# Cross-attention: the reciprocal of the second query tile's sums taken between the next pair's two maxima, not behind them

## The reference, cut to what matters

```python
q = q * scale
sim = jnp.einsum('bhid,bhjd->bhij', q, k)
attn = jax.nn.softmax(sim, axis=-1)
out = jnp.einsum('bhij,bhjd->bhid', attn, v)
out = out.transpose(0, 2, 1, 3).reshape(b, -1, INNER)
out = jnp.einsum('bnf,fd->bnd', out, Wout)
```

## Time and profile before

| what | value |
|---|---|
| median of 3 runs | 651.12 us (650.49 to 651.89) |
| the profiled execution's own time | 651.96 us |
| its span, from the first to the last instruction | 649.9 us |
| TensorE busy | 567.8 us, 87% |
| VectorE busy | 495.3 us, 76% |
| ScalarE busy | 419.7 us, 65% |
| GpSimd busy | 322.9 us, 50% |
| mean granted TensorE clock | 0.95 of full speed |

### The profile page before, as it was taken

One profiled execution on the slowest core, in us unless ns is written; L12 is line 12 of the kernel. 1 busy time (PEld: TensorE's weight loads), 2 busy tenths in 40 slices (PEclk: granted clock), 3 DMA queues, 4 the chain that ended last, 5 costly groups with the idle time before them and its releaser, 6 DMA issues. The chain is left out here.

```text
span 649.9 us, 11036 instructions
## 1 busy us (share of the span) xinstructions
PE 567.8 (87%) x3380; PEld 444.1 (68%) x3380; DVE 495.3 (76%) x1030; ACT 419.7 (65%) x1024; POOL 322.9 (50%) x606
## 2 busy tenths in 40 slices
PE   2959999999999889999987748899986599999996
PEld 1737868777677677787766636665554578888885
DVE  4757877886889587888689625998984479999995
ACT  2538777786767657777667415898883365656653
POOL 1345766785678765787667646466965100000000
PEclk9989999999999899999989865999998599999999
DMA  7020000000100000000000002002220000000001
GB/s 263 2 59 1 2 33 2 1 2 2 32 2 2 2 1 1 1 2 2 2 0 2 2 21 73 1 3 86 85 86 2 0 1 1 1 1 1 2 0 33
DMA packets 14393, 13.14 MB, mean 20 GB/s; under 512 B 2048, under 2 KB 13696, under 8 KB 14336
## 3 DMA queue, kind: packets, MB, share of 16 engines
q1 hardware_dynamic: 14032, 12.41, 6.0%
q10 hardware_dynamic: 304, 0.03, 0.0%
HBM read 11.92 MB, written 0.52 MB: 19 GB/s over the span
## 5 line engine op out<-in xcount | busy, mean ns | idle before, releaser
L1071 POOL TENSOR_SCALAR attn_probs<-attn_probs,rinv 128x512 f32<-128x512 f32 x128 | 87.4, 695 | 29.5 <-DVE rinv L975 29.5
L848 ACT ACTIVATE attn_probs<-bank,bias 128x512 f32<-128x512 f32 x128 | 87.3, 687 | 10.0 <-DVE bias L968 10.0
L984 DVE TENSOR_TENSOR pT_lo<-bank,pT_hi 128x512 fp32r<-128x512 f32 x128 | 87.4, 685 | 7.2 <-ACT pT_hi L864 5.8
L701 PE MATMUL bank<-ident,attn_probs 128*128 128x128 f32 x512 | 77.6, 285 | 12.5 <-POOL attn_probs L1071 11.8
L960 DVE TENSOR_REDUCE neg_max<-bank 128x1 f32<-128x512 f32 x128 | 82.0, 682 | 6.7 <-PE bank L686 6.7
L864 ACT ACTIVATE pT_hi<-bank 128x512 fp32r<-128x512 f32 x128 | 73.3, 594 | 15.3 <-PE bank L701 15.0
L701 PEld LDWEIGHTS bank<-ident,attn_probs 128*128 128x128 f32 x512 | 57.4, 143 | 36.5 <-POOL attn_probs L1071 21.0
L731 PE MATMUL bank<-pT_hi,vals 128*128 128x256 f32 x256 | 67.6, 295 | 2.2 <-DVE pT_lo L984 1.4
L731 PE MATMUL bank<-pT_lo,vals 128*128 128x256 f32 x256 | 65.6, 288 | 0.0
L1885 ACT ACTIVATE act_hi<-act_f 128x512 fp32r<-128x512 f32 x56 | 35.4, 633 | 43.4 <-DVE act_f L1926 43.3
L731 PEld LDWEIGHTS bank<-pT_hi,vals 128*128 128x128 f32 x256 | 49.9, 195 | 4.3 <-issue 1.7
(11 more groups left out here) (311 smaller groups left out, 1614.5 us busy)
## 6 DMA issues: line engine op xcount, KB each, us to landing
ctx_raw<-in_ctx SPq DMA_DIRECT2D x4, 512.0 KB, 4.8
wkv_raw<-in_L_xattn_Wkv SPq DMA_DIRECT2D x2, 1024.0 KB, 10.4
gu_raw<-in_L_ffn_w_gate SPq DMA_DIRECT2D x4, 448.0 KB, 3.6
gu_raw<-in_L_ffn_w_up SPq DMA_DIRECT2D x4, 448.0 KB, 4.4
dn_raw<-in_L_ffn_w_down SPq DMA_DIRECT2D x4, 448.0 KB, 5.4
x<-in_x SPq DMA_DIRECT2D x1, 512.0 KB, 6.8
wq_raw<-in_L_xattn_Wq SPq DMA_DIRECT2D x1, 512.0 KB, 10.3
wout_raw<-in_L_xattn_Wout SPq DMA_DIRECT2D x1, 512.0 KB, 12.1
```

Source lines behind the costliest of these rows:

```text
L701: last = pe.transpose(t_bank[half][:, j * N + t * P:j * N + (t + 1) * P], probs[:, g % 2, i, t, kt * P:(kt + 1) * P], k.ident[:, :])
L848: act.activation(probs[:, g % 2, i, t, :], score_bank(G, i)[:, :], ACT.Exp, bias=bias[:, t, h:h + 1], scale=X_SCALE, accum_out=row_sum[:, ...
L984: dve.tensor_tensor(pT_lo[:, i, 2 * half:2 * half + 2, :], t_bank[half][:, :].rearrange("p (j n) -> p j n", j=2), f(pT_hi[:, i, 2 * half:2 ...
L1071: pool.tensor_scalar(probs[:, g % 2, i, t, :], probs[:, g % 2, i, t, :], rinv[:, t, h:h + 1], 1.0, ALU.mult, ALU.mult).then_inc(p_norm_s, 1)
```

## The change

In VectorE's list the reciprocal of pair `s+1`, tile 1, moves ahead of one instruction: the second maximum of pair `s+2`, tile 0. Nothing else is touched; the instructions, their operands and their semaphores are the same.

```diff
                 probs_tail(s, 1, 0)
                 context_tail(s, 0)
                 maximum(s + 2, 0, 0)
+                inverse_sum(s + 1, 1)
                 maximum(s + 2, 0, 1)
-                inverse_sum(s + 1, 1)
                 shift(s + 2, 0)
                 context_tail(s, 1)
```

## The result

The changed kernel takes 646.67 us (median of 6 runs, 646.28 to 647.35) where the kernel before took 650.7 (median of 6 runs beside it): ratio 0.9938, 95% interval 0.9925 to 0.9951, a gain of 4.0 us. The forecast was 649.0 with a range down to 646.8: the sign was right, the size about half. The profiled execution took 646.28, with a span of 644.2 us (651.96 and 649.9 before).

The account below looks back on a forecast made before the run. TensorE was taken to bound the kernel, full in quiet steps, elsewhere waiting for GpSimd's normalisations. 1.00 + 1.10 + 0 + 0 + 0 = 2.1 us off 651.96 gave 649.9, and 649.0 for the median; range 646.8 to 651.5.

Parts of the forecast that it names:

- The chain at 187 us and its like: Early-sum steps at 187, 243, 329, 356 us: normalisation 0.60 us earlier, 0.35 reaching TensorE (0.30 at 356); 1.00 us together.
- 187 to 207 and 275 to 295: Three steps and their twin: an unstretched shift brings VectorE and the sum 0.33 us forward; about 0.55 us each, 1.10 together.
- 340, 347 and 356 us: 340 and 347 put at 0, between a gain of 0.13 + 0.45 and a loss of 0.2; 356 at 0.30 us.
- the prediction's nine waits, all for a normalisation: TensorE's cross-attention waits for GpSimd's normalisation: ten, 11.8 us in all; the last pair's 2.3 us left out.
- its bound of 0.60 for this step: At 356 us the step could give at most 0.60 us.
- Late sums at 0: In 14 steps GpSimd's sum is 0.3 us or more late; TensorE's backlog covers the late tail: 0, uncovered 9.4 us.
- The port: Moved shift falls among GpSimd's normalisations on the shared port, waits 0.12 us, ends with the first normalisation: 0.
- that rival (the shift behind the second normalisation): Each step's shift waits 0.66 us more: 656.7 us, or 653 if in a third of the steps; chance 0.11.
- The clock: Rival: shorter waits may keep TensorE at 2.4 GHz at 329 and 356 us, 0.83 + 0.43 us more; 647.3; chance 0.11.
- Its outer bound: No step gives more than the wait it has or 0.60 us, together 4.4 us off: 646.8.

Follow-up runs that it names:

- before_again: The kernel before, unaltered, run once more for a second profile: 650.17 us, ratio 0.9999.
- late_sums_only: Kernel before with the reciprocal moved only in the 14 pairs whose GpSimd sum is later than the first maximum: 652.16 us, ratio 1.0026.
- before_look1: The kernel before, unaltered, first of three more executions with a profile: 650.51 us.
- before_look3: The kernel before, unaltered, third of three more executions with a profile: 652.01 us.
- not_last_four: Kernel before with the reciprocal moved in all pairs but 27 to 30: 647.43 us, ratio 0.996.
- fill_all_before: Kernel before, old order, with unread matmuls filling TensorE's waits at pairs 14, 19, 22, 27 and 30: 649.06 us, ratio 0.9977.
- fill_long_waits: Kernel before, old order, with unread matmuls filling TensorE's waits at pairs 19, 27 and 30 alone: 649.3 us, ratio 0.9977.
- fill_waits: Kernel before, old order, with unread matmuls in TensorE's waits at pairs 27 and 30: 647.16 us, ratio 0.995.
- all_but_three: Kernel before with the reciprocal moved everywhere but in pairs 15, 23 and 28: 645.17 us, ratio 0.9921.
- after_look1: The changed kernel, unaltered, one more execution with its profile: 646.99 us.
- fill_all_after: Changed kernel with unread matmuls in what is left of TensorE's waits at pairs 14, 19, 22, 27 and 30: 646.87 us, ratio 0.9943.

## Why the prediction was half right

**The chain at 187 us and its like: right.** The prediction moved the normalisation 0.60 us, let 0.35 of it reach TensorE, and named the tail as the next late thing. Pairs 19 and 27 gave 0.36 to 0.42, and the second group of transposes starts 0.14 us behind the end of the tail, 185.72 to 185.86, as the 0.15 of the earlier trace rows had it.

**187 to 207 and 275 to 295: right in mechanism, a little too high.** The shift of 189.53 is no longer stretched (0.14 us at 188.03). It was not alone: where the prediction has "the others take 0.16", eleven shifts of the second tile took 0.44 to 0.67 us in the kernel before (pairs 5, 13, 15 to 17, 20, 21, 23 to 25, 28), each beside GpSimd's long subtraction, as this one of pair 16:

```profile
199.96 0.67 DVE L968 SCALAR_TENSOR_TENSOR bias<-neg_max,s0n 128x2 f32<-128x2 f32 x1
...
199.87 0.74 POOL L1101 TENSOR_TENSOR o_lo<-o_sum,o_hi 128x256 fp32r<-128x256 f32 x1
```

In the changed kernel all eleven take 0.14 to 0.15. The sum at pair 15 comes 0.37 us ahead of before_again's, net of the lead just before, where 0.33 was reckoned. But of that nothing is left for the second head of pair 15 (the prediction kept 0.10), and the three steps give 0.4 instead of 0.55.

**340, 347 and 356 us: right as a sum.** Pairs 28 and 29 lose 0.3 where 0 was put down, and pair 30 gains 0.6 to 0.8 where 0.30 was; together 0.3 to 0.5 for 0.30. At pair 30 a second wait nearly went, one for ScalarE ahead of the scores, 1.21 us in before_again and 0.26 in the changed kernel; the prediction's nine waits, all for a normalisation, didn't hold it, and its bound of 0.60 for this step was too low. In the timeline of TensorE of before_again:

```profile
352.15 0.50 PE L686 MATMUL bank<-keys_hi,q_hi 64*128 64x512 f32 x2 [1.21 <-ACT attn_probs L848]
354.40 1.09 PE L701 MATMUL bank<-ident,attn_probs 128*128 128x128 f32 x8 [1.28 <-POOL attn_probs L1071]
```

and of the changed kernel, where the transposes follow at 350.92 as shown above:

```profile
348.99 0.50 PE L686 MATMUL bank<-keys_hi,q_hi 64*128 64x512 f32 x2 [0.26 <-ACT attn_probs L848]
```

At 344.62 the shift takes 0.55 us and ends (345.17) with GpSimd's long subtraction (344.42 and 0.73). So do those of pairs 29 and 31 (0.52 and 0.55), where the old order had 0.15 at all three: the change has moved the collision from eleven pairs to these.

**Late sums at 0: false at three of the 14.** Two of the three were costed apart (197 and 285 us, where a tenth was to be kept, and 338, put at 0). Eleven are covered by TensorE's backlog, as the prediction had it. Where TensorE has none (at pairs 15 and 23 its wait is 0.02 to 0.04 us, at 28 it is 0.65) the late tail reaches it. The rows could have told: at 339.68 a wait of 0.77 stands, and at 197 the transposes start 1.02 us behind the reciprocal, which is the 0.25 and 0.75 of the bare chain at 187 and leaves no backlog.

**The port: right, at 0.** All 31 first-tile shifts behind a moved reciprocal take 0.18 to 0.19 us in the changed kernel's profile and end with the first normalisation, to 0.01 us: 184.93 and 0.18 is 185.11, and of the three normalisations that begin at 184.41 the first ends at 185.11. None missed its slot; that rival (the shift behind the second normalisation) is out. The Trainium skill (SBUF — State Buffer, "Who interferes with whom") has the one that starts first keep the port to its end; the trace agrees, 0.18 instead of 0.14 to 0.16 for a shift that meets the end of a normalisation, and 0.55 for the one at 344.62 that meets a subtraction begun 0.20 us before it. All fourteen stretched shifts of the two profiles start 0.09 to 0.30 us behind the start of such a subtraction and end 0.01 to 0.02 behind its end.

**The clock: the step that failed.** The sum holds nothing for the clock. The prediction saw it in the earlier trace rows (1.92 us for eight transposes at 329), priced it at 0.83 and 0.43, and made it a rival with a chance of 0.11, whose 647.3 came nearest to the 646.67 measured. Its outer bound, too, counts waits alone (and 4.4 us off 651.1 is 646.7, not 646.8). Three things were wrong in that. The price: a stretch at 1.2 GHz costs not only the transposes but all matmuls in it, 1.55 to 1.59 us at pairs 19 and 27 (the lead's fall from one pair to the next: 1.59 at pair 19 in late_sums_only, 1.58 in before_look1, 1.55 at pair 27 in before_look3). At pair 30 it is less clear: the second head's transposes fall back by 1.1 to 2.6 us, and of that 0.6 to 1.2 is left by pair 31 in four of the five executions that have the stretch and nothing in not_last_four, 0.6 on average. The places: the one profile had none at 243, where half of the executions have one. And the weight: a stretch in one profile was taken for something that may or may not go away, when the waits that bring it were just those that the change shortens. By the tally the old order loses, on average, 4/8 x 1.57 + 2/7 x 1.56 + 5/7 x 0.6 = 1.7 us behind these three waits, and the new one nothing. With the 1.5 to 1.9 us of the table this makes 3.2 to 3.6 of the 3.5 and 4.0 measured. The profiles of the two kernels themselves say the same without a tally: from pair 0 to pair 31 the five of the kernel before take 0, 0.3, 2.4, 2.4 and 2.8 us longer than before_again (itself the one with 0), 1.6 on average, and the three of the changed kernel take 1.9, 1.9 and 2.5 less, 2.1 on average: 3.7 us between them.

How far this is shown: that the open waits bring the stretches is shown by the fillings, which take away nothing but the waiting. From pair 0 to pair 31, fill_all_before and fill_long_waits take as long as before_again, the execution without a stretch behind these waits, to 0.3 us; fill_waits takes 1.1 longer, and it has the stretch at pair 19, which it does not fill. The size in whole times is less sure. The three gained 1.4, 1.1 and 3.1 us; the 1.7 lies in the intervals of the first two (0.1 to 2.9, 0.5 to 2.6), but the third, which fills only pairs 27 and 30 and should gain 0.9, gained 2.3 to 4.2 by its interval. By the mean it gained 2.3, with a standard error of 0.9, and its one profile is of the slowest of its six runs; why the median gained more stays open. A single time says little here: the kernel before took 647.3 to 652.9 us in one set of 18, and besides these stretches the start-up (up to 2.4 us) and what follows pair 31's last transposes (277.2 to 281.3 us over the 18 profiles) differ between executions.

## What to carry to other kernels

Here a wait of TensorE had two prices, its length and a stretch at half clock that may follow it; the second was about as large as the first, it came behind half of the long waits (11 of 22), and a single profile can miss it or show it. Before an edit that shortens waits is costed, look at more than one execution, note behind which waits the clock fell in any of them, and count every matmul in the stretch. And where an order is changed for all steps alike, sort the steps by what is late in each: of the 14 with a late sum here 11 lost nothing and 3 did, and leaving the three (645.2 us) or all 14 (645.0 us) as they were beats both kernels.

## What was not expected

In pair 17, ahead of its second head's transposes, TensorE waits 1.9 us for a layer norm's output, in either order. The clock of the matmuls behind that wait fell in all 10 profiles with the old order at pairs 14 and 16, in 3 of 5 with the new order at 14, 15 and 16, and in none of 3 that leave only pair 15 of them as it was. The same stretch as in the last of the changed kernel's windows above (clock 0.83), in all_but_three:

```profile
219.40:229.40 10.00, 8.22 (x57) 6.58 (x58) 6.05 (x13) 6.59 (x18) 7.42 (x16) 1.00 0.00 0
```

It is worth 1.2 us (the lead of all_but_three jumps from 0.83 to 2.02 between the two pairs), and with the 0.8 to 1.2 of the table it covers the 1.5 us by which all_but_three beats the changed kernel. The wait itself is as long in all of them. What decides is not shown. The shorter waits at pairs 14 and 16 go with fewer falls, 3 of 8 beside 10 of 10, but fill_all_before, which fills the wait at pair 14 in the old order, has the fall too. And that the three kernels without the move at pair 15 have none need not be owed to pair 15: of the eight profiles with the new order at 14 and 16, the three with the fall started up 0.7 to 1.4 us earlier than before_again, and the five without it at most 0.2 earlier, two of them with pair 15 moved (after_look1, and fill_all_after, which fills the wait at pair 14 too). In the old order the fall came whatever the start-up, from 0.5 later to 1.6 earlier.
